# Score maxima taken from two PSUM banks in one VectorE instruction

## What is computed

```python
scores = jnp.einsum('bhtd,bhsd->bhts', q, k)
probs = jax.nn.softmax(scores.astype(jnp.float32), axis=-1).astype(scores.dtype)
probs = probs.reshape(b, H, 2, t, t)
diff = probs[:, :, 0] - lam * probs[:, :, 1]
attn = jnp.einsum('bhts,bhsd->bhtd', diff, v)
```

## Time and profile before

| | |
|---|---|
| median of 3 runs | 5066.09 us |
| lowest and highest run | 5051.86, 5078.93 us |
| the profiled execution | 5038.04 us |
| its span in the profile | 5036.2 us |
| mean granted clock of TensorE | 0.987 of full |
| TensorE matmuls busy | 4882.4 us (97%) |
| VectorE busy | 3941.1 us (78%) |
| GpSimd busy | 2937.2 us (58%) |
| ScalarE busy | 2882.7 us (57%) |

### The profile page before, as it was taken

How to read it: one execution, slowest core, us unless ns; L and a number is a source line. 1 busy time by engine, 2 the same in 40 slices (tenths; PEclk the granted TensorE clock), 3 DMA queues, 4 the chain that set the end, 5 groups by cost and what they waited for, 6 DMA issues and landing times.

```text
span 5036.2 us, 67238 instructions
## 1 busy us (share of the span) xinstructions
PE 4882.4 (97%) x24784; PEld 1744.3 (35%) x24784; DVE 3941.1 (78%) x6295; ACT 2882.7 (57%) x5221; POOL 2937.2 (58%) x2134
## 2 busy tenths in 40 slices
PE   6999999999999999999999999999999999999999
PEld 2224242332423333242332424233242433324237
DVE  6988878888887878878888887888888788887526
ACT  1464646656465665646566464665646566564642
POOL 3583837757384674828568383765738477482740
PEclk7899999999999999999999999999999999999999
DMA  6121231303223130222312123230312313022117
GB/s 147 30 60 53 47 66 45 67 37 65 50 47 72 34 76 37 53 64 47 72 35 58 51 47 66 51 68 31 68 47 48 71 34 76 39 48 55 68 51 291
DMA packets 127723, 311.19 MB, mean 62 GB/s; under 512 B 27297, under 2 KB 30498, under 8 KB 113442
## 3 DMA queue, kind: packets, MB, share of 16 engines
q1 hardware_dynamic: 124178, 289.33, 24.2%
q10 hardware_dynamic: 3216, 17.57, 0.9%
HBM read 172.07 MB, written 99.61 MB: 54 GB/s over the span
## 4 chain that ended last, share of the span: by engine, by line
PE 78%; POOL 11%; ACT 5%; issue 3%; DVE 3%; DMA 0%; ACTq 0%; SPq 0%; DVEq 0%; POOLq 0%
PE s_ps L777 15%; PE o_ps L817 15%; PE st L804 14%; PE st L910 13%; POOL pair_sum L484 11%; PE sum_ps L832 8%; PE st L745 4%; PE st L763 4%; ACT probs L581 3%; PE st L987 2%; DVE neg_max L1107 2%; PE st L888 1%; PE o_ps L732 1%; PE s_ps L987 1%; PE sum_ps L732 0%
## 5 line engine op out<-in xcount | busy, mean ns | idle before, releaser
L484 POOL TENSOR_TENSOR pair_sum<-probs 128x512 f32<-128x512 f32 x2048 | 2829.0, 1416 | 1185.6 <-ACT probs L581 1185.6
L1107 DVE TENSOR_REDUCE neg_max<-s_ps 128x1 f32<-128x512 f32 x4096 | 2582.8, 682 | 705.5 <-PE s_ps L777 703.2
L581 ACT ACTIVATE probs<-st 128x512 f32<-128x512 f32 x4096 | 2161.3, 604 | 960.4 <-PE st L804 797.2
L777 PE MATMUL s_ps<-k_stack,q_stack 96*128 96x512 bf16 x4096 | 1518.6, 388 | 22.5 <-DVE neg_max L1107 21.0
L804 PE MATMUL st<-q_stack,k_stack 99*128 99x512 bf16 x4096 | 1473.3, 384 | 28.7 <-ACT probs L581 7.5
L817 PE MATMUL o_ps<-probs,values 128*32 128x512 f32 x8192 | 1092.4, 605 | 12.3 <-ACT probs L581 8.5
L804 PEld LDWEIGHTS st<-q_stack,k_stack 99*128 99x128 bf16 x4096 | 367.5, 97 | 1357.4 <-ACT probs L581 910.1
L777 PEld LDWEIGHTS s_ps<-k_stack,q_stack 96*128 96x128 bf16 x4096 | 400.3, 98 | 657.5 <-DVE neg_max L1107 315.3
L832 PE MATMUL sum_ps<-pair_sum,ones 128*32 128x512 f32 x4096 | 535.0, 594 | 27.3 <-POOL pair_sum L484 27.3
L910 PE MATMUL st<-pair_sum,weights 128*128 128x512 f32 x768 | 381.9, 594 | 11.8 <-ACT pair_sum L537 11.8
L531 ACT ACTIVATE probs<-st,gate_bias 128x512 f32<-128x512 f32 x192 | 131.6, 686 | 441.8 <-PE st L910 441.8
(11 more groups left out here) (151 smaller groups left out, 3042.2 us busy)
## 6 DMA issues: line engine op xcount, KB each, us to landing
q_stack<-qk_parts SPq DMA_DIRECT2D x384, 128.0 KB, 4.4
k_stack<-qk_parts SPq DMA_DIRECT2D x378, 128.0 KB, 7.0
swapped<-xa SPq DMA_DIRECT2D x128, 256.0 KB, 2.4
qk_parts<-swapped SPq DMA_DIRECT2D x64, 512.0 KB, 2.8
xa<-in_x SPq DMA_DIRECT2D x16, 1024.0 KB, 6.1
qk_parts<-low_part SPq DMA_DIRECT2D x64, 256.0 KB, 3.0
probs<-in_x SPq DMA_DIRECT2D x16, 1024.0 KB, 9.9
x_rows<-probs SPq DMA_DIRECT2D x16, 1024.0 KB, 3.8
```

The lines of the kernel that those rows point to most:

```text
L484: pool.tensor_tensor(pair_sum[q % 2][:, h, :], probs[a % 4][:, h, :], probs[(a + 1) % 4][:, h, :], ALU.add)\
L581: act.activation(probs[kk % 4][:, h, :], st[n % BANKS][:, :], ACT.Exp).then_inc(exp_done, 1)
L777: pe.matmul(s_ps[i % BANKS][:, :], q_stack[g][0:SROWS, s, t * P:(t + 1) * P], k_stack[g][0:SROWS, s, h * HALF:(h + 1) * HALF], start=True, ...
L1107: dve.tensor_reduce(neg_max2[:, at, i % 2:i % 2 + 1], s_ps[i % BANKS][:, :], AX.X, ALU.max, negate=True).then_inc(max_done, 1)
```

## The change

The three score banks become one PSUM tensor `scores`, so that one instruction can read two of them. The maximum of bank 0 is no longer taken when its score is ready: with the score of bank 1, one instruction of 128x2 from 128x1024 takes both, and counts `max_done` up by two. Bank 2 keeps its own instruction. Results are kept in the order of the scores, and `join_max` therefore needs two instructions, for the even and the odd sub-tiles, in place of one. The wait in `score` is as it was. Nothing else on any engine changes.

```diff
-        neg_max2 = sb("neg_max2", [P, SUBS * TT, 2])
+        neg_max2 = sb("neg_max2", [P, SCORES])
...
-        s_ps = [ctx.enter_context(nc.psum_tensor(f"s_ps{i}", [P, HALF], F32)) for i in range(BANKS)]
+        scores = ctx.enter_context(nc.psum_tensor("scores", [P, BANKS, HALF], F32))
+        s_ps = [scores[:, i, :] for i in range(BANKS)]
...
-                pe.wait_ge(max_all, u + 1)
+                pe.wait_ge(max_all, 2 * (u + 1))
...
             def maximum(u, i):
+                if i % BANKS == 0:
+                    return
+                n = 2 if i % BANKS == 1 else 1
                 dve.wait_ge(score_ready, SCORES * u + (i + 1))
-                at = SUB_ORDER[i // 16] * TT + i % 16 // 2
-                dve.tensor_reduce(neg_max2[:, at, i % 2:i % 2 + 1], s_ps[i % BANKS][:, :], AX.X,
-                                  ALU.max, negate=True).then_inc(max_done, 1)
+                dve.tensor_reduce(neg_max2[:, i + 1 - n:i + 1],
+                                  scores[:, i % BANKS + 1 - n:i % BANKS + 1, :], AX.X,
+                                  ALU.max, negate=True).then_inc(max_done, n)
...
             def join_max(u):
                 dve.wait_ge(max_done, SCORES * (u + 1))
-                dve.tensor_reduce(neg_max[:, 0:SUBS * TT], neg_max2[:, :, :], AX.X, ALU.min)\
-                   .then_inc(max_all, 1)
+                rows = neg_max[:, 0:SUBS * TT].rearrange("p (k two t) -> p two k t", two=2, t=TT)
+                halves = neg_max2[:, :].rearrange("p (two k t h) -> p two k t h", two=2, t=TT, h=2)
+                for sub in range(2):
+                    dve.tensor_reduce(rows[:, sub, :, :], halves[:, sub, :, :, :], AX.X, ALU.min)\
+                       .then_inc(max_all, 1)
```

## The result

The changed kernel takes 5426.3 us (median of 4 runs, 5425.6 to 5428.0) against 5065.4 for the kernel before (5051.9 to 5078.9): a ratio of 1.071, 95% interval 1.068 to 1.073. The prediction was 5390 us in a range of 5255 to 5450. The profiled executions are 5038 and 5426 us, 388 us apart where I had 324.

The account below looks back on a forecast made before the run. TensorE, working in order, was taken to bound the loops nearly everywhere. Fifteen sequences of 11.4 + 6.7 + 2.35 us (307), 12 for the last and 5 at the start gave 324, added to 5066: 5390 us, range 5255 to 5450.

Parts of the forecast that it names:

- The mechanism: In bursts with banks 1, 2, 0, bank 0's score waits for the pair: 24 scores, 13.2 and 7.8 us per loop.
- the short distance: Bank 1's score is one of two behind a burst's last key tile: bank 0's follows 0.65 us later, not 0.87.
- The size of each wait: Bank 0 comes free 1.69 us after bank 1's score starts, so bank 0's next score waits 0.82 or 1.04 us.
- (b): At score 45, g = 0, the 0.82 us wait is hidden, as TensorE then waits 1.34 us for GpSimd anyway.
- Outside the loops: Waits beside value projection (0.38 us twice), output projection (0.47) and last gates (1.12, score 9): 2.35 us a sequence.
- The first unit: Back-to-back reduces: three scores take 1.91 us instead of 1.80, 0.11 us for some 50 triples, 5 us.
- The old waits: Waits of 0.08 and 0.15 us in bursts of five go away: 1.0 us for g = 0, 1.1 for g = 1.
- The join: Two reduces of 64 elements replace one of 128, some 0.2 us longer, but covered before the transpose: costs nothing.
- that a pair is shorter or covered (1): Waits partly covered or pair 1056 ns: 65 us less each, 5325, both 5260; chance 0.10 below the forecast.
- that it takes as long as two (3): The two-bank instruction takes 1364 ns or more, each of 27 waits 0.15 us longer: 5450 us; chance 0.03 above the forecast.
- that VectorE is the bound (2): VectorE is the hidden bound, so waits for maxima go away: 32 us less, 5034 us; chance 0.05.
- no difference (4): VectorE's relief and the waits cancel, which needs waits under 0.1 us each; chance 0.03.

Follow-up runs that it names:

- 9: Kernel before, with each maximum over only the first 256 of its bank's 512 columns: 4970.7 us, 0.985 of the kernel before.
- 1: Kernel before's one reduce per bank, with the new order of results and the join in two reduces: 5042.9 us, 1.000 of the kernel before.
- 2: Changed kernel, but banks 0 and 1 get two one-bank reduces issued together, only the second counting, by two: 5423.0 us, 1.075 of the kernel before.
- 3: Changed kernel, but banks 0 and 1 get two one-bank reduces issued together, each counting for itself: 5182.3 us, 1.027 of the kernel before.
- 7: Changed kernel, but the two-bank reduce reads only the first 256 columns of each bank: 5159.4 us, 1.020 of the kernel before.
- 5: Changed kernel, but with one reduce per bank in the first two units: 5384.7 us, 1.067 of the kernel before.
- 6: Changed kernel, but bank 0 is reduced alone and banks 1 and 2 together: 5541.7 us, 1.095 of the kernel before.
- 4: Changed kernel, pairing only where no bank 0 score waits, one reduce per bank elsewhere and at the start: 5089.4 us, 1.009 of the kernel before.

## Why the prediction was right, and where it was short

**The bound** was read rightly: TensorE in order, VectorE a follower (9). **The mechanism** was right, and in place: of the 24 scores that the two lists of counts named, all 24 waited in the trace of the changed kernel, each of the six with the short distance 1.11 us and the others 0.89 (0.97 once). Experiments 1, 2, 3 and 7 vary the hold with nearly all else kept (7 also reads half of the columns), and the cost follows. With bank 0 free 1.77 us after bank 1's score it is 1.071 to 1.075, with about 1.2 us 1.020 to 1.027, and without a hold 1.000.

**The figure** looks closer than the sum was. The sum gave 324 us and the traces have 388, so 64 are missing. I added it to a median that lay 28 us above the profiled execution of the kernel before. The changed kernel has no such distance (5426.0 in the profile, 5426.3 as the median), and so 5390 is only 36 us short. These 28 us are luck.

**The size of each wait** was 0.07 us too small, 0.82 and 1.04 for 0.89 and 1.11. The pair's length is right to 8 ns; what failed is the step that took the 0.42 us from a score to its reduce from a one-bank reduce. For a two-bank one it is 0.486 (the median of 1068 from the third unit on, in the changed kernel, where VectorE stood idle). 24 x 0.07 is 1.7 us a sequence, 25 us in all.

**The cover at score 45** was there and did not help. The wait of 1.5 us for GpSimd behind it is gone from the trace, as (b) of the sum says, but one of 0.69 is new and another has grown to 1.13 us, and TensorE's waits for GpSimd's sums are 23 us in all after 27 before. In a period the sums over keys give nothing back: they start 0.3 us later in all. Taking (b) out, 0.8 us a sequence, would have brought the sum nearer.

**Outside the loops** I had 2.35 us a sequence, and at those four scores the trace has 0.47 (score 9), 0.46 and 0.47 (99 and 102) and 0.47 (111), 1.9 in all. Score 9 is the miss: the pair was not held up by the cell's products. Two waits that I had not seen came in their place, 0.47 us at score 27 and 0.30 at score 3, so 2.6 us in all.

**The first unit** was the largest miss: 44 us up to the second transpose, where I had 5 and one loop of 11.4. The term that was mis-sized is the cycle of 1.91 us for three scores: its 0.22 and 0.42 us were of the full clock, and this stretch runs at 0.50, where they are 0.40 and 0.74 and the cycle 2.42 (5). The windows' granted clock would have told me.

**The old waits** that go away (1.0 and 1.1 us) did go. **The join** cost nothing (1). Of the signs that I had named, the period was 321.2 us for 318.7, TensorE's wait for maxima 377 us for "over 250", and VectorE's busy time fell by 158 us for "some 100": 72 at the reduces, less than the 95 to 200 that I had for them, and 105 at its 310 rope steps, which I had not expected to change. Why they are shorter I did not test.

Rivals: that a pair is shorter or covered (1) and that it takes as long as two (3) fell with the 1223 ns and the 24 waits; that VectorE is the bound (2) with experiment 9; no difference (4) with the result. The rule of the Trainium skill that stands under rival 2 ("VectorE: DVE Perf Modes", "The TRN2 errata") held for the instruction, as 1223 ns in place of 2 x 682 saves 141 where its estimate had 124, and decided nothing.

## What to carry to other kernels

An instruction that takes two buffers in one gives both back when it ends: before merging, take the time from the last use's start to the release and set it against the distance to the producer's next turn, at every place in its order. Saved time on an engine that stands idle between its inputs is worth little (here 71 us of 942), and what it costs is paid by the engine that waits. When two engines begin to take turns, work with the clock that is granted in that stretch, and look which reduces change their place in the list.

## What the runs showed of the hardware

- A VectorE reduce that reads two PSUM banks starts 0.067 us later after the matmul that it waits for: 0.486 us for 0.419 at the full clock. With 512 elements in two banks it is 0.485 (7) and with two rows in one bank 0.418 (8), so it goes with the second bank, not with length or rows. Why, the traces do not say.
- Two engines that take turns can cost more than their waits: 3.2 us of an idle TensorE were followed by 7 us at a granted clock of 0.52, and such a drop stands there in all 15 sequences (6).
- A VectorE addition with two SBUF inputs took 5.56 us in place of 1.87 beside GpSimd's additions, in 5 of 14 otherwise equal periods, and 5.91 to 6.20 us in five places of three other runs (4).
